# Where the distance bias of a two-layer attention kernel is added: TensorE matmuls or VectorE, with three queues reordered

## The reference

```python
def _L1_attn_ref(hidden_states, Wq, Wk, Wv, Wo, bo):
    H, G, DQ, DV = (16, 4, 128, 128)
    q = (hidden_states @ Wq).reshape(N, t, H, DQ).transpose(0, 2, 1, 3)
    k = (hidden_states @ Wk).reshape(N, t, G, DQ).transpose(0, 2, 1, 3)
    v = (hidden_states @ Wv).reshape(N, t, G, DV).transpose(0, 2, 1, 3)
    q = _rope(q); k = _rope(k)              # x * cos + rot * sin
    k = jnp.repeat(k, REP, axis=1); v = jnp.repeat(v, REP, axis=1)
    scores = jnp.einsum('bhtd,bhsd->bhts', q, k)
    scores = scores + _alibi(t)[None]       # -|i - j| * 2 ** (-(h + 1) / 2)
    scores = scores / math.sqrt(DQ)
    scores = 30.0 * jnp.tanh(scores / 30.0)
    scores = jnp.where(causal[None, None], scores, -jnp.inf)
    probs = jax.nn.softmax(scores, axis=-1)
    ctx = jnp.einsum('bhts,bhsd->bhtd', probs, v)
    return ctx.transpose(0, 2, 1, 3).reshape(N, t, H * DV) @ Wo + bo
```

## Time and profile before

| | us |
|---|---|
| median of 3 runs (539.3 to 541.05) | 540.04 |
| the profiled execution | 537.99 |
| its span, first to last instruction | 535.8 |
| TensorE busy | 501.2 (94%) |
| VectorE busy | 377.3 (70%) |
| ScalarE busy | 338.9 (63%) |
| GpSimd busy | 294.7 (55%) |

### The profile page before, as it was taken

The page is one execution under the profiler, slowest core; times in us unless marked ns, Lnnn a source line. Parts: engine busy times, 40 slices in busy tenths (PEclk is TensorE's granted clock), DMA queues, the critical chain, the costliest instruction groups (busy, mean ns, idle before and its releaser), DMA issues.

```text
span 535.8 us, 10729 instructions
## 1 busy us (share of the span) xinstructions
PE 501.2 (94%) x3600; PEld 437.3 (82%) x3600; DVE 377.3 (70%) x825; ACT 338.9 (63%) x755; POOL 294.7 (55%) x291
## 2 busy tenths in 40 slices
PE   7989999999999998799975879999999999999995
PEld 6768888888888787588854778999999999999884
DVE  2589888888885356755555788779766986678656
ACT  4457777777776655444432588778766876686673
POOL 4746777677775226336560577677544665465330
PEclk8999999999999999799996989999999999999999
DMA  8917999970000292345575000000000000000001
GB/s 265 393 64 281 323 314 329 332 252 0 0 0 1 94 410 79 105 132 160 166 256 187 1 1 2 0 1 2 1 1 2 0 1 2 1 2 1 1 21 60
DMA packets 17613, 56.79 MB, mean 106 GB/s; under 512 B 2612, under 2 KB 12346, under 8 KB 15770
## 3 DMA queue, kind: packets, MB, share of 16 engines
q1 hardware_dynamic: 14816, 49.81, 27.1%
q0 software_dynamic: 2752, 6.40, 3.6%
HBM read 49.19 MB, written 28.45 MB: 145 GB/s over the span
## 4 chain that ended last, share of the span: by engine, by line
PE 77%; DVE 8%; ACT 5%; issue 4%; POOL 3%; DMA 3%; SPq 0%; DVEq 0%; POOLq 0%; ACTq 0%
PE bank L442 10%; PE bank L444 10%; PE bank L443 10%; PE bank L990 5%; PE bank L585 5%; PE bank L507 5%; PE bank L610 3%; PE bank L587 2%; PE bank L734 2%; PE bank L1007 2%; PE bank L719 2%; PE bank L721 2%; PE bank L720 2%; PE bank L621 2%; PE bank L701 2%
## 5 line engine op out<-in xcount | busy, mean ns | idle before, releaser
L1099 ACT ACTIVATE probs<-bank,neg_max,q_scale 128x256 f32<-128x256 f32 (+1 forms) x128 | 63.8, 508 | 38.4 <-DVE neg_max L1742 38.4
L1951 POOL TENSOR_TENSOR probs<-probs,inv_sum 128x512 f32<-128x512 f32 x64 | 51.6, 828 | 44.3 <-DVE inv_sum L1750 44.3
L1984 POOL TENSOR_TENSOR exps<-exps,tables 128x256 f32<-128x256 f32 x32 | 24.6, 769 | 71.8 <-ACT exps L1209 71.7
L1209 ACT ACTIVATE exps<-bank 128x768 f32<-128x768 f32 x32 | 25.9, 809 | 41.3 <-PE bank L701 41.3
L1971 POOL TENSOR_TENSOR swapped<-swapped,tables 128x512 f32<-128x512 f32 x32 | 43.1, 1350 | 10.0 <-ACT swapped L1130 9.8
L1565 DVE TENSOR_TENSOR q_lo<-q_sum,q_hi 128x512 fp32r<-128x512 f32 x32 | 27.2, 851 | 29.7 <-ACT q_hi L1163 29.5
L2084 POOL DMA_INDIRECT y_rows<-y_slot,dest x31 | 29.7, 959 | 29.9 <-issue 19.1
L1728 DVE TENSOR_TENSOR swapped<-bank,tables 32x512 f32<-32x512 f32 x64 | 44.4, 694 | 1.4
L1943 POOL TENSOR_TENSOR qT<-qT,swapped 128x512 f32<-128x512 f32 x32 | 40.8, 1276 | 7.1 <-DVE swapped L1728 7.1
L442 PE MATMUL bank<-x,wq_hi 128*128 128x256 f32 x128 | 38.5, 301 | 3.2 <-DVE q_sum L1552 3.2
L585 PE MATMUL bank<-keysT,qT 128*128 128x256 f32 x128 | 38.3, 381 | 0.0
(11 more groups left out here) (283 smaller groups left out, 1774.2 us busy)
## 6 DMA issues: line engine op xcount, KB each, us to landing
slots<-in_c_unused SPq DMA_DIRECT2D x20, 1036.0 KB, 36.4
gu_all<-in_gate_up SPq DMA_DIRECT2D x4, 1024.0 KB, 7.9
xg<-slots SPq DMA_DIRECT2D x31, 129.5 KB
wvo_raw<-in_wvo SPq DMA_DIRECT2D x1, 2560.0 KB, 20.8
dn_all<-in_down SPq DMA_DIRECT2D x1, 2048.0 KB, 7.7
wq_full<-in_Wq SPq DMA_DIRECT2D x1, 2048.0 KB
wo_raw<-in_Wo SPq DMA_DIRECT2D x1, 2048.0 KB
wqk_raw<-in_wqk SPq DMA_DIRECT2D x1, 1536.0 KB, 10.4
```

The source lines that it names most:

```text
L1099: ins = act.activation(probs[:, par, h, c0:c1], bank[:, 2 * par + h, c0:c1], ACT.Exp, bias=neg_max[:, par, i:i + 1], scale=q_scale[:, b, t ...
L1951: ins = pool.tensor_tensor(some, some, inv, ALU.mult)
```

## The change

The bias matmuls go. A table `distance` of minus |i - j| times the slopes of heads 0 and 1 is loaded once in float32, and VectorE adds it, times a power of two, to the scores while it moves them from PSUM to SBUF (`add_bias`: one instruction of 512 columns and one of 256). Tanh then works in place in SBUF, and the next scores wait for `biased` instead of `capped`. The addition of the rope parts moves from VectorE to GpSimd for all but the first three units. ScalarE's turn becomes tanh(n), swap(n + 3), context_hi(n - 2), q_hi(n + 2), exp(n); VectorE's add_bias(n), q_lo(n + 1), cos(n + 3), norm(n - 1), context_lo(n - 2), extras.

```diff
@@ setup
-    alibi_keys = sb("alibi_keys", [P, T], BF16)
-    alibi_queries = sb("alibi_queries", [P, H, T], BF16)
+    zeros_bf = sb("zeros_bf", [P, T], BF16)
+    distance = sb("distance", [P, 2, T])
@@ def pe_scores1(eng, n):
         if n:
-            eng.wait_ge(at1["capped"], n)
+            eng.wait_ge(at1["biased"], n)
...
-            three_pass(eng, dst, ..., True, False)
-            mm = eng.matmul(dst, alibi_keys[:, keys], alibi_queries[:, 2 * p:2 * p + 2, queries],
-                            start=False, stop=True, skip_group_check=True)
+            mm = three_pass(eng, dst, ..., True, True)
@@ def act_layer1(act):
+        act_swap_queries(act, 2)
         act_query_hi(act, 1)
-        act_swap_queries(act, 2)
         for n in range(B * PAIRS + 2):
             b, u = divmod(n, PAIRS)
             if b < B:
-                act.wait_ge(at1["scores_done"], n + 1)
-                if n >= 2:
-                    act.wait_ge(at1["ctx_done"], n - 1)
-                act.activation(exps[:, n % 2, :], scores1, ACT.Tanh, ...).then_inc(at1["capped"], 1)
+                act.wait_ge(at1["biased"], n + 1)
+                act.activation(exps[:, n % 2, :], exps[:, n % 2, :], ACT.Tanh, ...).then_inc(at1["capped"], 1)
+            if n + 3 < B * PAIRS:
+                act_swap_queries(act, n + 3)
+            if 2 <= n < B * PAIRS:
+                context_hi(n)
             if n + 2 < B * PAIRS:
                 act_query_hi(act, n + 2)
-            if n + 3 < B * PAIRS:
-                act_swap_queries(act, n + 3)
-            if b < B and n + 2 >= B * PAIRS:
-                context_hi(n)
             if b < B:
                 act.wait_ge(at1["masked"], n + 1)
                 act.activation(..., ACT.Exp, scale=30.0).then_inc(at1["exp_done"], 1)
...
-            if n >= 2 and not (b < B and n + 2 >= B * PAIRS):
+            if n >= B * PAIRS:
                 context_hi(n)
@@ def dve_layer1(dve, counted, n_step):
+        def add_bias(n):
+            slope = 2.0 ** -(n % PAIRS)
+            dve.wait_ge(at1["scores_done"], n + 1)
+            if n == 0:
+                dve.wait_ge(ld["alibi_in"], 32)
+            if n >= 2:
+                dve.wait_ge(at1["ctx_done"], n - 1)
+            dve.scalar_tensor_tensor(out=pair_view(exps[:, n % 2, 0:2 * T]), in0=distance[:], scalar=slope,
+                                     in1=pair_view(scores1[:, 0:2 * T]), op0=ALU.mult, op1=ALU.add)
+            dve.scalar_tensor_tensor(out=pair_view(exps[:, n % 2, 2 * T:3 * T]), in0=distance[:, :, 0:P], scalar=slope,
+                                     in1=pair_view(scores1[:, 2 * T:3 * T]), op0=ALU.mult,
+                                     op1=ALU.add).then_inc(at1["biased"], 1)
...
         query_cos(2)
-        query_lo(1)
         query_sum(2)
         for n in range(B * PAIRS + 2):
...
-            if n + 2 < B * PAIRS:
-                query_lo(n + 2)
+            if b < B:
+                add_bias(n)
+            if n + 1 < B * PAIRS:
+                query_lo(n + 1)
             if n + 3 < B * PAIRS:
                 query_cos(n + 3)
             if 1 <= n < B * PAIRS + 1:
                 context_norm(n - 1)
-            if n + 3 < B * PAIRS:
-                query_sum(n + 3)
             if n >= 2:
                 context_lo(n - 2)
@@ def pool_layer1(pool):
-        def sin_queries(m):
+        def turn_queries(m):
             pool.wait_ge(at1["swap_done"], m + 1)
             sw = pair_view(swapped[:, m % 2, :])
             pool.tensor_tensor(sw, sw, sin_rows(), ALU.mult).then_inc(at1["sin_done"], 1)
+            if m >= 3:
+                pool.wait_ge(at1["sin_done"], m + 1)
+                pool.wait_ge(at1["cos_done"], m + 1)
+                pool.wait_ge(at1["q_summed"], m)
+                pool.tensor_tensor(q_sum[:, m % 2, :], q_sum[:, m % 2, :], swapped[:, m % 2, :],
+                                   ALU.add).then_inc(at1["q_summed"], 1)
@@ GpSimd, start of the kernel
-        pool.memset(alibi_keys[:], 0.0).then_inc(ld["cleared"], 1)
-        pool.memset(alibi_queries[:], 0.0).then_inc(ld["cleared"], 1)
+        pool.memset(zeros_bf[:], 0.0).then_inc(ld["cleared"], 1)
...
-        pool.wait_ge(ld["cleared"], 2)
-        pool.wait_ge(su["warmed"], 1)
-        pool.dma_start(alibi_queries[0:6], a["c_alibi_queries"]).then_inc(ld["alibi_in"], 16)
-        pool.dma_start(alibi_keys[0:6], a["c_alibi_keys"]).then_inc(ld["alibi_in"], 16)
+        pool.dma_start(distance[:], a["c_distance"]...).then_inc(ld["alibi_in"], 16)
```

More of the change, by code:

```diff
@@ L71, in shape_constants @@
     maskT = np.concatenate([later.T, later.T], 1)
-    def parts(x):
-        out, rest = [], x.astype(np.float32)
-        for _ in range(3):
-            hi = ((rest.view(np.uint32) + np.uint32(0x8000)) & np.uint32(0xFFFF0000)).view(np.float32)
-            out.append(hi)
-            rest = (rest - hi).astype(np.float32)
-        return out
     slopes = np.float32(2.0) ** (-np.arange(1, H + 1, dtype=np.float32) * np.float32(8.0) / np.float32(H))
     slopes = slopes.astype(np.float32)
-    query_rows = parts(np.ascontiguousarray(np.broadcast_to(slopes[:, None], (H, T))))
-    query_rows += parts((-slopes[:, None] * pos[None, :]).astype(np.float32))
-    alibi_queries = np.stack(query_rows, 0)
-    alibi_keys = np.stack([pos] * 3 + [np.ones(T, np.float32)] * 3, 0)
+    distance = np.abs(pos[None, None, :] - pos[0:P, None, None]) * -slopes[None, 0:2, None]
     part, expert = np.arange(P), np.arange(E)
@@ L98, in shape_constants @@
     triangles = np.concatenate([part[:, None] < part[None, :], np.ones((P, P))], 1)
-    out = dict(c_ident=np.eye(P, dtype=np.float32), c_mask=mask, c_alibi_keys=alibi_keys,
-               c_alibi_queries=alibi_queries, c_route=route, c_unused=unused, c_triangles=triangles,
+    out = dict(c_ident=np.eye(P, dtype=np.float32), c_mask=mask, c_distance=distance.reshape(P, 2 * T),
+               c_route=route, c_unused=unused, c_triangles=triangles,
                c_key_tables=np.concatenate([key_cos.reshape(P, 2 * ROPE), key_sin.reshape(P, 2 * ROPE)], 1),
@@ L293, in build @@
               "latents lat_done latT_hi_done latT_lo_done q_scaled keyT_done keysT_copied fold_done "
-              "fold_scaled fold_T_done fold_q_copied fold_o_done fold_o_copied rope_cols warmed")
+              "fold_scaled fold_T_done fold_q_copied fold_o_done fold_o_copied rope_cols")
     ln = sems("norm", "xT_done xT_hi_done xT_lo_done y_done y_read var_ready sqrt_done x_new var_second")
@@ L308, in build @@
                "ctx_copied max_step max_ready probs_ready probsT_done probsT_copied")
-    at1 = sems("a1", "q_done swap_done cos_done sin_done q_summed q_hi q_ready scores_done capped masked exp_done "
+    at1 = sems("a1", "q_done biased swap_done cos_done sin_done q_summed q_hi q_ready scores_done capped masked exp_done "
                "ctx_done ctx_norm ctxT_done c_hi c_lo out_done")
@@ L481, in pe_logits @@
             if b == 1 and t == 0:
-                eng.wait_ge(ld["alibi_in"], 48)
+                eng.wait_ge(ld["alibi_in"], 32)
             eng.matmul(dst, ones_bf, marks[:, t:t + 1, :].broadcast_to([P, 2, E]), start=False, stop=False,
@@ L498, in keep_busy @@
         for i in range(n):
-            mm = pe.matmul(bank[:, 7, 0:T], alibi_keys[:, 0:P], alibi_keys[:], start=True, stop=True)
+            mm = pe.matmul(bank[:, 7, 0:T], zeros_bf[:, 0:P], zeros_bf[:], start=True, stop=True)
         return mm
@@ L698, in pe_scores1 @@
             keys, queries = slice(tile * P, tile * P + P), slice(tile * P, T)
-            three_pass(eng, dst, k_hi[:, b % 2, p // 2, keys], k_lo[:, b % 2, p // 2, keys],
-                       q_hi[:, n % 4, :, queries], q_lo[:, n % 4, :, queries], True, False)
-            mm = eng.matmul(dst, alibi_keys[:, keys], alibi_queries[:, 2 * p:2 * p + 2, queries],
-                            start=False, stop=True, skip_group_check=True)
+            mm = three_pass(eng, dst, k_hi[:, b % 2, p // 2, keys], k_lo[:, b % 2, p // 2, keys],
+                            q_hi[:, n % 4, :, queries], q_lo[:, n % 4, :, queries], True, True)
         mm.then_inc(at1["scores_done"], 1)
@@ L915, in _ @@
         pe.wait_ge(ld["cleared"], 1)
-        keep_busy(pe, WARM[0]).then_inc(su["warmed"], 1)
+        keep_busy(pe, WARM[0])
         pe.wait_ge(su["wa_hi"], 1)
@@ L1998, in pool_layer1 @@
         for m in range(3):
-            sin_queries(m)
+            turn_queries(m)
         for n in range(B * PAIRS):
@@ L2007, in pool_layer1 @@
             if n + 3 < B * PAIRS:
-                sin_queries(n + 3)
+                turn_queries(n + 3)
             if 1 <= n <= PAIRS:
@@ L2029, in _ @@
         pool.dma_start(mask_bf[:], a["c_mask"]).then_inc(ld["bf_in"], 16)
-        pool.wait_ge(ld["cleared"], 2)
-        pool.wait_ge(su["warmed"], 1)
-        pool.dma_start(alibi_queries[0:6], a["c_alibi_queries"]).then_inc(ld["alibi_in"], 16)
```

(4 more changed lines are left out.)

2 lines of the change are left out of this document (1 added, 1 removed).

## The result

The changed kernel took 556.50 us (median of 4 runs, 555.72 to 560.41), the kernel before on the same chip 539.72 us (4 runs, 539.30 to 541.05): slower. The ratio on record is 1.0345, 95% interval 1.0299 to 1.0392; the two medians alone give 1.031. The forecast was 551.5 us against 540.04, a ratio of 1.021, and its range ended at 557, which is 1.031. The profiled execution is the one of 555.72 us. It is 17.7 us longer than the profiled one of before (537.99), where the sum had 12.8.

A forecast was written before the change was run, and what follows sets the result against it. A round trip between VectorE and ScalarE in every unit, with extras behind it, replaces TensorE as the bound. Head, loops and tail put unit 29's exponential 12.8 us later: 537.99 + 12.8 = 550.8, forecast 551.5 us, range 545 to 557.

The forecast's parts named there:

- Rival 2: Layer 1: the loop binds only in units with long extras, others give it back; 540 to 542 us, chance 0.12.
- Rival 1: Layer 1: TensorE stays the bound, with shorter units; about 532 to 534 us, chance 0.24.
- The price of add_bias: VectorE: the 512- and 256-column bias instructions take 0.61 and 0.42 us, 1.03 us from start to end.
- rival 3: VectorE: add_bias is slowed by GpSimd, 0.3 to 0.9 us more a unit; 559 to 575 us, chance 0.04 with rival 4.
- The bare loop: Layer 1 unit without extras, from add_bias through tanh, swap, cos, norm and context_lo: 5.08 us.
- the head: Start of layer 1, from the last query matmul before unit 0 at 302.1 us to add_bias(2) at 319.85 us.
- The sum of the loops: Layer 1, all loops with their extras from add_bias(2) to add_bias(29): 194.6 us.
- u = 0: experts and statistics 3.54: VectorE's extras in units u = 0 add 3.54 us, making the loop 8.6 us, or 9.2 with the binary weights' low part.
- u = 4, 6: k_hi, then k_lo: 6.0: Units u = 4 and 6: k_hi, then k_lo end the loop at 6.0 us, in the first batch 6.6.
- The key units: Units u = 3 and 5: ScalarE's key swap, GpSimd's key sines, then keys_sum; 8.4 us, in the first batch 9.7.
- The tail: After unit 29's exponential: durations unchanged, the bias of units 30 and 31 hidden behind ScalarE's table loads.
- rival 4: TensorE's clock falls as it waits more; 8 us more if layer 1 ran at 0.95; chance 0.04 with rival 3.

The follow-up runs named there:

- experiment 1: Changed kernel with add_bias taken out (distance bias left out), tanh reading the scores from PSUM: 531.17 us, ratio 0.9884.
- experiment 8: Changed kernel with VectorE's extras and key sums put behind add_bias and q_lo, ahead of cos: 539.55 us, ratio 1.0038.
- experiment 9: Kernel of experiment 8 with the long jobs (expert rows, binary weights, a normalisation) spread over turns: 532.71 us, ratio 0.9921; again on another chip 531.57 us.
- experiment 10: Kernel of experiment 9 with norm ahead of cos on VectorE: 532.35 us, ratio 0.9870.
- experiment 6: Changed kernel with GpSimd's rope sum cut short, from 512 to 8 columns: 550.38 us, ratio 1.0241.

## Why the prediction was off, and what in it was right

**What bounds the kernel: right.** The forecast was that a round trip VectorE, ScalarE, VectorE in every unit replaces TensorE as the bound, and that the extras stand behind it. The windows, the 30 waits of cos for the swap, and experiments 1 and 8 show it: without add_bias the changed order is 8.9 us faster than before in layer 1; with it, and the extras out of the loop, nearly all of the loss is gone. Rival 2 needed loops 0.4 us shorter than worked out; they were 0.23 longer (6.15 / 27). Rival 1 named 532 to 534 us, and with the bias on VectorE only experiments 9 and 10 came there. Its condition, 1.0 us off every unit, was stricter than needed: the loops of experiment 9 sum to 177.7 us, 0.62 us a unit less than the forecast's 194.6.

**The price of add_bias: right.** 0.68 and 0.41 us, 1.03 from start to end. The longest of its 32 wide instances took 0.69 us, and the four that ran wholly beside GpSimd 0.67 to 0.68, so rival 3, add_bias slowed by GpSimd, falls. Cos, which has one input in PSUM too, ran beside GpSimd in 30 of 32 units and never took more than 0.69.

**The bare loop, the head and TensorE's saving: right.** 5.15 against 5.08 us, 17.87 against 17.9 (the mask of the head ends by its rows at 309.2, not 309.4, a small slip), and 0.39 against 0.35 us a unit.

**The sum of the loops: too small by 6.15 us, and this is the step that failed.** The path was the one described; two terms of the sum were too small. They make 6.3 us, other units add 1.5, and the key units gave 1.65 back.
- "u = 0: experts and statistics 3.54": the four additions were taken at the 2.61 us of before, although the forecast itself moved 1.3 us of GpSimd work a unit beside them. They took 4.67 us in unit 8. The loop was 10.77 instead of 8.6, 2.2 us of the error; with the short sum it was 8.78.
- "u = 4, 6: k_hi, then k_lo: 6.0": 6.48 in the later batches, of which experiment 6 gives 0.33 to GpSimd beside k_lo; the other 0.15 is the exponential that came at 4.15 instead of 4.0. In the first batch 7.7 instead of 6.6, where k_lo took 1.73 us beside wo_lo; with the short sum it took 0.69 and the loop 6.66.

Both are one omission, and of the 6.3 us experiment 6 gives 5.4 to it. The forecast noted that the rope sum took 1.00 us beside GpSimd and 0.69 alone, used it to bound add_bias, which wasn't slowed, and put it at nothing for the instructions with SBUF inputs that stayed on VectorE.

**The key units: right size by luck.** "GpSimd's key sines 6.45 to 7.75" had the sines wait for the query sum. In the second and third batch they waited for ScalarE's key swap, which came at 6.2 instead of 5.95, and the sum was done by then. 8.4 forecast, 8.2 to 8.3 measured. Experiment 6, whose expectation rested on the wrong cause, missed by it. In the first batch, where the split of the output weights stands between sum and sines, GpSimd's queue did hold them up: 9.7 forecast, 9.13 and 9.18 measured, 8.7 with the short sum or with the sum on VectorE.

**What TensorE waits for: wrong in part.** I named gaps ahead of turn, released by context_lo; there are two such waits, 2.0 us in all. The gaps ahead of the scores, released by q_lo, are there (9.3 us, 8 times), but the largest were not named: TensorE waited for cos ahead of the queries (11.9 us, 19 times). As the loops set the time, it changed no number.

**The tail: "what they were" was off by 1.0 us.** The bias of unit 30 was hidden behind a table load; that of unit 31 wasn't. In the changed kernel VectorE holds c_lo, the normalisation and the shift ahead of it, and tanh waits:

```profile
528.16 0.69 DVE L1564 TENSOR_TENSOR c_lo<-bank,c_hi 128x512 fp32r<-128x512 f32 x1 [1.96 <-ACT c_hi L1173]
...
528.96 0.74 DVE L1415 TENSOR_SCALAR x_rows<-x_rows,moments,inv_dev 128x256 f32<-128x256 f32 x2
...
529.88 0.69 DVE L1575 SCALAR_TENSOR_TENSOR exps<-distance,bank 128x512 f32<-128x512 f32 x1
```

```profile
530.93 0.84 ACT L1192 ACTIVATE exps<-exps 128x768 f32<-128x768 f32 x1 [0.93 <-DVE exps L1577]
```

Experiments 8 and 9 moved that work behind the bias. In experiment 9 tanh of unit 31 follows the exponential without a wait, and the tail is 30.1 us, as before the change (30.5 in experiment 8):

```profile
503.46 0.85 ACT L1201 ACTIVATE exps<-exps 128x768 f32<-128x768 f32 x1 [1.03 <-POOL exps L2002]
504.21 0.83 ACT L1192 ACTIVATE exps<-exps 128x768 f32<-128x768 f32 x1
```

**The clock (rival 4): small, but there.** The granted clock was 0.98 over 330 to 500 us, not 1.00, and fell to 0.92 and 0.84 in slices at and after those in which TensorE was busy for 6.0 and 6.7 of 10 us. I expected it to stay. What that cost in the changed kernel was not separated: the loop, not TensorE, sets the time there.

## What to carry to other kernels

An engine with a quarter of its time free may still have no room for a step that makes it wait for another engine and be waited for in the same turn. Write down the loop of waits first, then put every job with no deadline in this turn into the idle stretch inside that loop, and cut the ones that don't fit: here the same instructions in another order made 556.5 us into 532. And when work moves to GpSimd, look at every VectorE instruction with both inputs in SBUF that will run beside it, and at every `tensor_scalar` out of SBUF, not only at those that are new; what each lost here was about what was left of GpSimd's instruction.
